# Router logits of the second loop from the plain transposed tokens, corrected per token by mean and reciprocal root

## What is computed

```
mu = mean(x); var = mean((x - mu)**2)
h = (x - mu) * rsqrt(var + 1e-05) * ln_gamma + ln_beta
logits = h @ Wr + br                    # Wr: [128, 8]
probs = softmax(logits)
pre = x @ W1s + b1s ; act = gelu(pre) ; y = act @ W2s + b2s      # per expert, on x itself
out = sum over experts of probs * y
```

## Time and profile before

| | |
|---|---|
| median of 3 runs | 1858.81 us (1850.88, 1858.81, 1859.11) |
| the profiled execution | 1854.63 us, span 1852.9 us |
| mean granted TensorE clock | 0.951 |
| busy: PE, DVE, ACT, POOL | 88%, 72%, 62%, 56% of the span |
| second loop | about 446 to 1380 us |

### The profile page before, as it was taken

How to read it: one execution, slowest core, us unless ns; L and a number is a source line. 1 busy time by engine, 2 the same in 40 slices (tenths; PEclk the granted TensorE clock), 3 DMA queues, 4 the chain that set the end, 5 groups by cost and what they waited for, 6 DMA issues and landing times. The chain is left out here.

```text
span 1852.9 us, 43667 instructions
## 1 busy us (share of the span) xinstructions
PE 1635.7 (88%) x15584; PEld 1265.7 (68%) x15584; DVE 1336.8 (72%) x4587; ACT 1140.6 (62%) x2772; POOL 1046.1 (56%) x1598
## 2 busy tenths in 40 slices
PE   7988988997999999999999999999878999499920
PEld 4666666666877777787777777776656777399920
DVE  6788888865678888888888888988647884711127
ACT  2566666553788887787788877776314775144412
POOL 4477777753346666666666666666531533175275
PEclk8999999999999999999999999999879999599965
DMA  4111111102000000000000000000023220355222
GB/s 102 50 49 56 56 56 56 52 9 87 15 1 2 1 7 8 2 7 9 7 9 7 9 7 2 5 5 9 4 59 108 92 86 21 102 76 79 55 65 85
DMA packets 80222, 70.23 MB, mean 38 GB/s; under 512 B 16000, under 2 KB 67082, under 8 KB 79882
## 3 DMA queue, kind: packets, MB, share of 16 engines
q1 hardware_dynamic: 74730, 56.33, 10.0%
q0 software_dynamic: 4608, 9.45, 3.5%
q10 hardware_dynamic: 672, 1.67, 0.2%
HBM read 26.52 MB, written 13.63 MB: 22 GB/s over the span
## 5 line engine op out<-in xcount | busy, mean ns | idle before, releaser
L2293 POOL TENSOR_SCALAR probs<-probs,rsums 128x128 f32<-128x128 f32 (+1 forms) x512 | 209.3, 429 | 287.2 <-DVE rsums L2190 286.5
L1056 POOL TENSOR_SCALAR at_least<-magnitudes,candidates 128x512 bf16<-128x512 f32 x128 | 198.7, 1569 | 90.1 <-DVE candidates L941 90.1
L1911 ACT ACTIVATE probs<-probs,low 128x130 f32<-128x130 f32 (+1 forms) x512 | 227.7, 461 | 6.4 <-DVE low L2174 6.3
L2174 DVE CUSTOM_DVE_ANT_0 probs<-dist,pq,nmin 128x128 f32<-128x128 f32 (+1 forms) x512 | 181.3, 409 | 65.6 <-PE pq L1627 64.2
L1013 DVE TENSOR_REDUCE negmax<-ps_scores 128x4 f32<-128x1024 f32 x128 | 155.8, 1217 | 37.8 <-PE ps_scores L632 36.6
L810 ACT ACTIVATE pT<-ps_scoresT 128x1024 f32<-128x1024 f32 x128 | 131.2, 1025 | 78.4 <-PE ps_scoresT L640 74.8
L2184 DVE COPY pT<-pq 128x384 f32<-128x384 f32 x256 | 130.1, 549 | 3.9 <-PE pq L1642 3.9
L1822 ACT ACTIVATE qn<-pq 128x512 f32<-128x512 f32 x128 | 77.2, 603 | 72.0 <-PE pq L1484 70.3
L3315 POOL DMA_INDIRECT m_x<-token_rows,m_idx_put x80 | 75.8, 947 | 80.1 <-DVE m_idx_put L3245 33.4
L1627 PE MATMUL pq<-k1T,q1T 64*128 64x128 f32 (+1 forms) x1024 | 119.3, 351 | 0.5 <-ACT k1T L1837 0.4
L3267 DVE COPY m_y<-pm 128x256 f32<-128x256 f32 x40 | 17.0, 425 | 139.9 <-PE pm L3153 139.9
(11 more groups left out here) (546 smaller groups left out, 5035.9 us busy)
## 6 DMA issues: line engine op xcount, KB each, us to landing
qkT<-qk_parts SPq DMA_DIRECT2D x48, 256.0 KB, 2.6
cqT<-cq_parts SPq DMA_DIRECT2D x24, 256.0 KB, 2.5
expert_answers<-m_y SPq DMA_DIRECT2D x40, 128.0 KB, 2.0
m_w<-in_L_ffn_moe_w_dram SPq DMA_DIRECT2D x16, 256.0 KB, 5.8
ckT<-ck_parts SPq DMA_DIRECT2D x24, 128.0 KB, 2.6
x<-in_x_dram SPq DMA_DIRECT2D x16, 128.0 KB, 2.2
...
```

The costliest lines, as they stand in the source:

```text
L1056: pool.tensor_scalar(at_least[:, a, :], mags[:, 512 * (a // 2):512 * (a // 2) + 512], cf[:, a:a + 1], None, ALU.is_ge).then_inc(mask_ready ...
L1911: ins = act.activation(probs[:, a, keys_nulls(i, w)], probs[:, a, keys_nulls(i, w)], ACT.Exp, bias=low[:, a, i:i + 1], scale=-1.0, accum_o ...
L2174: ins = dve.tensor_tensor_reduce(probs[:, a + t, keys(i, w)], dist[:, (1 - t) * P:N], ps[:, t * P:t * P + w], slopes[h], nmin[u][:, t, h:h ...
L2293: ins = pool.tensor_scalar(probs[:, a + t, keys(i, w)], probs[:, a + t, keys(i, w)], rsums[:, a + t, i:i + 1], 1.0, ALU.mult, ALU.mult)
```

## The change

The layer norm is pulled out of the matmul. With g = gamma, b = beta, s the reciprocal root and m the mean of a token,

```diff
-            def h_T(u):
-                pe.wait_ge(*xn0_ready.at(NT * (u + 1)))
-                transpose_tiles(u, "hT", xn0, 0.5)
+            def router_rows(u):
+                if u:
+                    return
+                pe.wait_ge(parts_ready, 1)
+                ps = ring.open(pe, "router_rows", held=1.4)
+                pe.matmul(ps[:, 0:NE0], ones_f, wr_ln[:, 0:NE0], start=True, stop=True)
+                pe.matmul(ps[:, NE0:2 * NE0], ones_f, wr_ln[:, NE0:2 * NE0], start=True, stop=False)
+                pe.matmul(ps[:, NE0:2 * NE0], ones[:], bias_parts[:, 3 * D:3 * D + NE0], start=False, stop=True)\
+                    .then_inc(ring.filled("router_rows"), 1)
...
             def router(u):
-                if u == 0:
-                    pe.wait_ge(first_loaded, 16 * len(first_loads))
-                    pe.wait_ge(parts_ready, 1)
-                ring.wait_read(pe, "hT", u)
                 ps = ring.open(pe, "logits", u, held=0.9)
                 for t in range(NT):
-                    o = ps[:, t * NE0:(t + 1) * NE0]
-                    pe.matmul(o, hT[:, t * P:(t + 1) * P], wr[:], start=True, stop=False)
-                    mm = pe.matmul(o, ones[:], bias_parts[:, 3 * D:3 * D + NE0], start=False, stop=True)
+                    mm = pe.matmul(ps[:, t * NE0:(t + 1) * NE0], xT[:, t * P:(t + 1) * P], wr_ln[:, 0:NE0],
+                                   start=True, stop=True)
                 mm.then_inc(ring.filled("logits", u), 1)
...
-                affine(hT[:], ps[:, 0:N], ln_f).then_inc(ring.read("hT", u), 1)
-
             def logits_exp(u):
-                ring.wait_read(act, "logits", u)
+                act.wait_ge(*logits_ready.at(u + 1))
...
                 ring.wait_read(dve, "b2T")
+                for i in range(2):
+                    chain.add(dve.tensor_scalar(wr_ln[:, i * NE0:(i + 1) * NE0], wr[:], ln_f[:, i:i + 1], None, ALU.mult))
+                chain.add(dve.memset(ones_f, 1.0))
                 three_parts(dve, chain, bias_parts[0:3, :], bias_rows, bias_work, pick)
...
             def logits(u):
+                if u == 0:
+                    ps = ring.wait(dve, "router_rows")
+                    chain.add(dve.tensor_scalar(route_rows[:, 0:NE0], ps[:, 0:NE0], -1.0, None, ALU.mult))
+                    link(dve.tensor_copy(route_rows[:, NE0:2 * NE0], ps[:, NE0:2 * NE0]))
+                    dve.sem_inc(ring.read("router_rows"), 1)
+                dve.wait_ge(*root_ready[0].at(u + 1))
                 ps = ring.wait(dve, "logits", u)
-                l = ps[:, 0:NT * NE0].rearrange("p (t e) -> p t e", t=NT)
-                link(dve.tensor_reduce(pr[:, :, 0], l, AX.X, ALU.max))
-                dve.tensor_tensor(lg[:], l, pr[:, :, 0:1].broadcast_to([P, NT, NE0]), ALU.subtract)\
-                    .then_inc(ring.read("logits", u), 1)
+                for t in range(NT):
+                    dve.scalar_tensor_tensor(lg[:, t, :], route_rows[:, 0:NE0], mv[0][u][:, t, 0:1],
+                                             ps[:, t * NE0:(t + 1) * NE0], ALU.mult, ALU.add).then_inc(logits_read.sem, 1)
+                dve.wait_ge(*logits_read.at(NT * (u + 1)))
+                dve.sem_inc(ring.read("logits", u), 1)
+                for t in range(NT):
+                    ins = dve.scalar_tensor_tensor(lg[:, t, :], lg[:, t, :], root[0][u][:, 2 * NT + t:2 * NT + t + 1],
+                                                   route_rows[:, NE0:2 * NE0], ALU.mult, ALU.add)
+                    chain.add(ins)
+                dve.wait_ge(chain.sem, chain.n)
+                link(dve.tensor_reduce(pr[:, :, 0], lg[:], AX.X, ALU.max))
+                dve.tensor_tensor(lg[:], lg[:], pr[:, :, 0:1].broadcast_to([P, NT, NE0]), ALU.subtract)\
+                    .then_inc(logits_ready.sem, 1)
```

24 lines of the change are left out of this document (11 added, 13 removed).

## The result

The changed kernel takes **1851.49 us** (median of 20 runs, 1845.71 to 1859.95), the kernel before 1857.45 us in 20 runs beside them (1850.88 to 1862.77). The ratio is 0.9976, with a 95% interval of 0.9965 to 0.9987: 4.5 us less, or 2.4 to 6.5 (the two medians lie 6.0 us apart). The forecast was 1848.5 us in a range of 1840 to 1858. The time lies in the range and within 0.5% of no change, but the forecast stands 0.55% under the 1858.81 us that it started from, twice the gain that was measured.

A forecast was written before the change was run, and what follows sets the result against it. TensorE, issuing without holes in the second loop, was taken as the bound. Gains of 3.8 us steady and 2.8 filling, 6.8 with small extras, off 1854.6 or 1855.9 gave 1847.8 or 1849; forecast 1848.5 us, range 1840 to 1858.

The forecast's parts named there:

- The whole second loop: All gains in the second loop: 3.8 us steady plus 2.8 filling, 6.8 with the small gain at three filling items' logits.
- the steady part: Items 6 to 15 of the second loop: 0.38 us gained per item, 3.8 us in all.
- The start of the sum: Time the gain was subtracted from: profiled run 1854.6 us giving 1847.8, or mean of four 1855.9 giving 1849.
- (a): TensorE, step of hT: two transposes and the wait for the second score bank go, 0.37 us per item.
- R4: Rival: bank order was counted, not seen; if v still waits for the second score bank, 1852 us; chance 0.10.
- (b): TensorE, step of logits: its start does not move, the block shortens by 0.04 us per item, at most 0.09.
- (c): ScalarE: one 128x256 affine per item goes; worth 0, as TensorE does not wait for ScalarE in the steady stretch.
- (d): VectorE, logits step: added multiply-adds and waits cost 0.9 us, making it 0.4 late; TensorE stall 0.03 us (0 to 0.7).
- R3: Rival: VectorE paces the step after logits because two-tensor operations wait for GpSimd; 1863 us, half of it 1857; chance 0.12.
- (e): Pipeline filling: 2.8 us gained (0 to 4); 0.9 from item 5, 0.6 from items 3 and 4, 1.3 earlier.
- R1: Rival: TensorE's half-clock stretch moves, worth 3.3 us; gain to 1845 us, chance 0.12, or loss to 1852, chance 0.06.
- The signs named beforehand: Trace readings in the second loop that would show the forecast right, such as a 16-step period of 105.1 to 105.3 us.

The follow-up runs named there:

- first profile: First profiled execution of the changed kernel, nothing else altered; 1857.82 us itself, 64 steady steps in 419.51 us, median of its 20 runs 1851.49 us.
- the third: The changed kernel profiled and timed a third time, nothing altered; 64 steady steps in 419.19 us, median of 12 runs 1850.81 us, ratio to before 0.9978.
- the second: The changed kernel profiled and timed again, nothing altered; 64 steady steps in 417.90 us, median of 6 runs 1849.90 us, ratio to before 0.9950.
- the kernel with the old order: Changed kernel with the bank planner told a bank is taken for half a step at hT's old place, restoring the earlier bank order; 1865.16 us (1 run).
- null keys first: Changed kernel with the null keys' normalisation moved ahead of the first logits on VectorE, in the start-up only; 1859.05 us (1 run).
- in the bank: Changed kernel with VectorE's multiply-adds writing to the logits' own bank, and maximum and subtraction reading it; 1850.11 us (12 runs), ratio to before 0.9965.
- The kernel with the correction left out: Changed kernel without VectorE's mean and root correction of the router products, so routing weights are wrong; 1848.03 us (1 run).

## Why the prediction was right or wrong

**The whole second loop** came out as forecast, by a sum whose parts were off both ways. From VectorE's first operation to the last scores it took 867.96 us before and 861.50 in the changed kernel's first profile, 6.5 less; in the third 6.9 less, in the second 9.6 less. The forecast was 6.8. In the first profile the steady part and the run-out gave 5.6 instead of 3.8 + 0.2, and the filling 0.9 instead of 2.8. That the total agrees is luck.

**The start of the sum** is the step that failed for the headline. I took the gain off the profiled run and off a mean of four runs, 1855.9, and then compared with a median of 1858.81. Of the 10.3 us between 1858.81 and 1848.5 only 6.8 were worked out; the other 3.5 are the choice of the start. Twenty runs of before have a median of 1857.45; less 6.8 that is 1850.65, 0.8 us from the time measured. With three runs shown that differ by 8 us, the number to start from was open by several microseconds, and I gave it no term of its own. The first loop alone differs by up to 9.7 us from run to run in its clock. So the forecast point was a gain of 0.55% against the time given, where the working supported 0.35 to 0.4% and the runs gave 0.24%, 0.50% and 0.22% on three occasions.

**(a)** Mechanism right, size off: 0.37 forecast, 0.53 found. The wait for the second score bank goes because the bank order shifts: the kernel with the old order has it back (R4 falls, and its reasoning, that everything hangs on the banks, holds). Too long were the 0.06 for a semaphore that no longer delays anything, and the four records of `null`, 0.37 with no wait in front and not 0.44. The 0.29 for the transposes was 0.22; the pause behind them belonged to the wait.

**(b)** 0.04 is what the bias matmuls cost by themselves. The step gained 0.12, since the router starts 0.09 sooner, which I had excluded with "its start does not move".

**(c)** Right in the steady part. In the start-up ScalarE's wait for the logits holds other work behind it; in the changed kernel TensorE still meets no wait from it, and only with the logits 2.1 us later (null keys first) did it wait 1.58 us.

**(d)** The step of the mechanism that was mis-sized most. The chain was too short as worked out: in the bank, where no operation reads two SBUF tensors, the same six operations take 1.17 us and not 0.97, since the multiply-adds of a pair start 0.14 apart and not 0.08 like the RECIPROCALs. In the changed kernel the block takes 1.28 to 1.33 in the fast items; that this equals 0.97 + 0.3 is an accident, since the 0.3 was meant for the lock. VectorE is then 0.14 to 0.19 late and not 0.4, and TensorE doesn't stall. In the slow items the block takes 2.33, VectorE is 0.66 late, and the stall is 0.26 instead of 0.03. I had the cause, from the earlier trace rows, and R3 had its place and the slack of 0.45: 0.66 - 0.45 = 0.21, close to the 0.26 found. But I averaged the lock into a flat 0.3 us, though it comes whole or not at all, and though the subtraction would stand next to GpSimd's scalings of 1.05 us and not to those of 0.43.

What kept the lateness below the growth of the block, and R3 at its full size (1863) away, are the two `y` operations behind it, which I had taken as fixed or growing. They end with the same GpSimd scalings and so give back what the block takes: 1.41 us for the two before, 1.07 to 1.17 in fast items, 0.59 in slow ones, where GpSimd has finished (its second scaling ends at 741.52). Before, in the second profile of the changed kernel, and in its first:

```profile
736.37 1.41 DVE L2026 TENSOR_SCALAR y<-l_r,l_moments,l_roots 128x128 f32<-128x128 f32 x2
...
738.82 1.07 DVE L2026 TENSOR_SCALAR y<-l_r,l_moments,l_roots 128x128 f32<-128x128 f32 x2
...
741.79 0.59 DVE L2026 TENSOR_SCALAR y<-l_r,l_moments,l_roots 128x128 f32<-128x128 f32 x2
```

**(e)** 2.8 us forecast. 0.9 found: item 5 gave 0.94 (the step fell from 6.78 to 5.84), as forecast; the steps 0 to 16 gave 0.34 (94.97 to 94.63), where items 3 and 4 were to give 0.6; up to the first scores 0.39 were lost, where items 0 to 2 were to gain 1.3. There my statement that queued matmuls cover the longer first routing was wrong. The first logits take VectorE 1.4 us longer and the null keys behind them end 1.1 later, so TensorE comes 0.46 later to their transposes; it then waits 1.00 for GpSimd's `xn`, because the `xn` of VectorE whose going I priced as a gain had kept VectorE's subtractions off GpSimd's way. `k` starts 30.72 us into the loop instead of 30.09, and the pause ahead of `x1T` ends at 51.31 instead of 50.65. The kernel with the correction left out has 30.03 for `k`, so the correction makes that delay; its pause still ends at 50.97, and what makes this rest was not tried.

**Not forecast:** 0.2 us every second item in steps 4 and 5. Before, in those items the small copy in front of VectorE's scores takes 1.07 us; in the kernel in the bank it takes 0.18:

```profile
689.96 1.07 DVE L2167 COPY probs<-nneg 128x8 f32<-128x8 f32 x1
...
693.50 0.18 DVE L2182 COPY probs<-nneg 128x8 f32<-128x8 f32 x1
```

The kernel with the correction left out still has the loss (5.70 and 7.22 instead of 5.63 and 7.08), every kernel with the correction has not. So VectorE being 0.13 us or more later may move this copy out of GpSimd's way. That is inferred from these rows; it was not tried by itself.

**R1.** In the changed kernel's first profile the half clock of the filling stayed behind the same pause, as in the earlier trace rows:

```profile
503.00:509.00 6.00, 5.57 (x22) 5.09 (x23) 3.79 (x8) 4.00 (x6) 3.53 (x5) 0.50 0.00 0
```

In later profiles it also fell elsewhere, for kernels that do the same there. It is part of the spread between runs rather than of the change. My price of 3.3 us for it was too high: without the drop the first scores come some 0.5 to 0.9 sooner (71.29 to 71.43 instead of 71.95 to 72.17), and a drop behind them makes the steps 0 to 16 some 0.5 to 1.8 us longer (95.08 to 96.46 instead of 94.63).

**The signs named beforehand** mostly speak against the working. The period is 104.95, below the 105.1 to 105.3; `v` starts 0.21 after the end of the pair ahead, where I wrote 0.5 (my own sum gives 0.34); the first L1592 comes 0.47 after the first router matmul, near the 0.44; VectorE is 0.66 late and not at most 0.5; TensorE waits 0.16 in the second `k` group and not at most 0.1; and two-tensor operations of over 0.7, a sign of being wrong, are there with 0.95.
